# Spreading the LayerNorm factor over the partitions: two transfers through DRAM, or transposes on TensorE

## The reference, cut to what matters

```
xn     = (x - mean(x)) / sqrt(var(x) + 1e-5)              # per token (row)
q      = lora_proj(xn, Wq...);  k, v = lora_proj(ctx, ...) # 16 heads of 16
scores = q*0.25 @ k^T + bias                               # bias: [128, 16, 128, 128] f32
x      = x + tanh(g_xattn) * softmax(scores) @ v
t      = layernorm(x);  e = argmax(softmax(t @ Wg + bg))   # one of 8 experts
x      = x + tanh(g_ffn) * (gelu(t @ W1[e] + b1[e]) @ W2[e] + b2[e])
```

## Time and profile before

| | |
|---|---|
| time, median of 3 runs (lowest, highest) | 2027.51 us (2027.22, 2029.68) |
| time of the profiled execution | 2017.96 us |
| its span, first to last instruction | 2016.1 us |
| mean granted TensorE clock | 0.835 of full speed |
| busy: PE, DVE, ACT, POOL | 69%, 48%, 38%, 49% |
| DMA, mean over the span | 143 GB/s |

### The profile page before, as it was taken

One profiled execution on the slowest core, in us unless ns is written; L12 is line 12 of the kernel. 1 busy time (PEld: TensorE's weight loads), 2 busy tenths in 40 slices (PEclk: granted clock), 3 DMA queues, 4 the chain that ended last, 5 costly groups with the idle time before them and its releaser, 6 DMA issues.

```text
span 2016.1 us, 45866 instructions
## 1 busy us (share of the span) xinstructions
PE 1390.3 (69%) x12568; PEld 1158.6 (57%) x12568; DVE 974.1 (48%) x5961; ACT 772.7 (38%) x1660; POOL 997.8 (49%) x1051
## 2 busy tenths in 40 slices
PE   5656666676766666766656666767665666999998
PEld 3445545554655455555545555656554555788887
DVE  3334445443544444444444444545444444756555
ACT  1334434343433343443333343434333343533333
POOL 2334545554545445554445444545445445655555
PEclk7778878888877788877878887878787888999999
DMA  4454556555556565566556555665555654688896
GB/s 113 125 119 126 132 126 132 101 130 131 131 111 123 127 122 113 124 131 131 111 122 131 129 114 116 130 131 131 125 111 129 127 115 107 214 289 281 276 284 215
DMA packets 156795, 289.27 MB, mean 143 GB/s; under 512 B 36836, under 2 KB 72166, under 8 KB 156544
## 3 DMA queue, kind: packets, MB, share of 16 engines
q1 hardware_dynamic: 142992, 252.02, 55.1%
q0 software_dynamic: 12624, 34.62, 4.6%
q10 hardware_dynamic: 1056, 1.39, 0.2%
HBM read 251.89 MB, written 36.98 MB: 143 GB/s over the span
## 4 chain that ended last, share of the span: by engine, by line
DMA 69%; PE 14%; SPq 9%; issue 6%; DVE 1%; ACT 0%; POOLq 0%; POOL 0%; DVEq 0%; ACTq 0%
DMA rs_dram<-x2n 68%; PE bank L788 6%; PE bank L802 6%; SPq L402 5%; SPq L366 2%; PE bank L776 1%; DMA x_sb<-in_x 1%; DMA RS<-rs_dram 1%; DVE sc L1042 1%; SPq L356 0%; PE bank L595 0%; PE bank L629 0%; PE bank L620 0%; SPq L384 0%; SPq L379 0%
## 5 line engine op out<-in xcount | busy, mean ns | idle before, releaser
L1042 DVE CUSTOM_DVE_ANT_0 sc<-bank,sc 128x128 f32<-128x128 f32 x2048 | 443.9, 286 | 264.3 <-PE bank L595 133.7
L484 POOL TENSOR_TENSOR sc<-sc,rowmax 128x1024 f32<-128x1024 f32 x256 | 480.0, 1896 | 156.9 <-DVE rowmax L1042 148.7
L595 PE MATMUL bank<-KT,QT 32*128 32x256 f32 x2048 | 195.6, 509 | 476.0 <-DVE QT L1101 443.9
L595 PEld LDWEIGHTS bank<-KT,QT 32*128 32x128 f32 x2048 | 119.7, 238 | 511.5 <-DVE QT L1101 373.3
L506 POOL TENSOR_SCALAR ve<-mv 128x2 f32<-128x2 f32 (+1 forms) x135 | 31.5, 233 | 674.3 <-DVE mv L1065 649.9
L620 PE MATMUL bank<-cst,sc 128*128 128x128 f32 x2048 | 291.6, 289 | 1.2 <-issue 1.2
L886 ACT ACTIVATE PT<-bank 128x512 f32<-128x512 f32 x512 | 281.6, 604 | 17.6 <-PE bank L620 14.1
L620 PEld LDWEIGHTS bank<-cst,sc 128*128 128x128 f32 x2048 | 243.2, 149 | 35.0 <-issue 34.7
L1052 DVE BATCH_NORM_STATS2 st<-x_sb 128x6 f32<-128x256 f32 x128 | 53.7, 419 | 399.6 <-DMA x_sb<-in_x 399.5
L852 ACT ACTIVATE QT<-QT,cst 128x256 f32<-128x256 f32 x128 | 58.0, 501 | 444.8 <-DVE QT L1101 444.8
L645 PE MATMUL bank<-XT,wq 128*128 128x256 f32 x512 | 148.0, 439 | 115.0 <-DVE rowmax L1042 114.5
(11 more groups left out here) (148 smaller groups left out, 2157.1 us busy)
## 6 DMA issues: line engine op xcount, KB each, us to landing
sc<-in_bias SPq DMA_DIRECT2D x256, 512.0 KB
w_sb<-in_w SPq DMA_DIRECT2D x69, 257.0 KB, 3.9
CT<-in_w SPq DMA_DIRECT2D x69, 256.0 KB, 4.0
xg<-rows_dram SPq DMA_DIRECT2D x63, 272.0 KB, 3.9
x_sb<-in_x SPq DMA_DIRECT2D x128, 128.0 KB, 11.1
CT<-in_ctx_in SPq DMA_DIRECT2D x64, 256.0 KB
XT<-in_x_turned SPq DMA_DIRECT2D x64, 256.0 KB
RS<-rs_dram SPq DMA_DIRECT2D x128, 64.0 KB
```

Source lines behind the costliest of these rows:

```text
L484: nc.gpsimd.tensor_tensor(s, s, m, ALU.subtract).then_inc(sub_ok, 1)
L595: ins = mm(b_s[j][:, 2 * P * c:2 * P * c + 2 * P], QT[rows, pair, c, P * sq:P * sq + P], KT[rows, pair, c, sq].rearrange("p e k -> p (e k) ...
L1042: ins = nc.vector.tensor_tensor_reduce(out=s, in0=b_s[q][:, P * (h % 4):P * (h % 4) + P], in1=s, scale=1.0, scalar=LOWEST, op0=ALU.add, op ...
```

## The change

The two transfers, the DRAM tensor rs_dram and the semaphores rs_out and rs_in go. In each even step TensorE makes two transposes, for the two sequences of the pair, of the factor's column repeated 128 times (a broadcast access pattern), into the second half of bank b_x, once the semaphore rs_ok says that GpSimd has written both factors. ScalarE copies the 128x256 result to RS, which now has one buffer. V, which uses the same bank, waits for that copy (rs_evac), and so does `scale_queries`.

```diff
-            def send_scale(t):
-                sp.wait_ge(rs_ok, t.n(1, 1))
-                sp.nop(nofuse=True)
-                sp.dma_start(rs_dram[t.n()], ln[:, (t.k - 7) % 8, 0, 0:1]).then_inc(rs_out, 16)
-
-            def spread_scale(t):
-                pair = t.k // 2 % 2
-                if t.reached(4):
-                    sp.wait_ge(scaled_ok, t.per(2, 1, -1))
-                    sp.nop(nofuse=True)
-                sp.wait_ge(rs_out, t.n(16, 16))
-                sp.nop(nofuse=True)
-                tok = P * t.slot(2)
-                sp.dma_start(RS[:, pair, tok:tok + P], rs_rows[t.n()].partition_broadcast(P)).then_inc(rs_in[pair], 16)
...
@@ PE, step @@
+                if qry and qry.slot(2) == 0:
+                    pe.wait_ge(rs_ok, qry.n(1, 2))
+                    if not cur and val.reached(1):
+                        pe.wait_ge(v_evac, val.n())
+                    for n in range(2):
+                        rs = ln[:, (qry.k + n - 7) % 8, 0, 0:1].broadcast_to([P, P])
+                        ins = nc.tensor.transpose(b_rs[:, P * n:P * n + P], rs, ident)
+                    ins.then_inc(rs_ready, 1)
...
-                    if not cur and val.reached(1):
+                    if qry and qry.slot(2) == 0:
+                        pe.wait_ge(rs_evac, qry.per(2, 1, 1))
+                    elif not cur and val.reached(1):
                         pe.wait_ge(v_evac, val.n())
@@ ACT, step @@
+                if qry and qry.slot(2) == 0:
+                    act.wait_ge(rs_ready, qry.per(2, 1, 1))
+                    nc.scalar.copy(RS[:], b_rs).then_inc(rs_evac, 1)
@@ DVE, scale_queries @@
-                dve.wait_ge(rs_in[pair], t.per(4, 32, 32))
+                dve.wait_ge(rs_evac, t.per(2, 1, 1))
```

More of the change, by code:

```diff
@@ L106, in sem @@
             return ctx.enter_context(nc.semaphore(name))
-        rs_dram = nc.dram_tensor("rs_dram", (N, P, 1), F32, kind="Internal").ap()
-        rs_rows = rs_dram.rearrange("n p a -> n a p")
         rows_dram = nc.dram_tensor("rows_dram", (DUMMY + FT, ROW), F32, kind="Internal").ap()
@@ L136, in flamingo_block @@
         sc = sb("sc", [P, 4, HEADS * P])
-        RS = sb("RS", [P, 2, 2 * P])
+        RS = sb("RS", [P, 2 * P])
         XT = sb("XT", [P, 2, KC, 2 * P])
@@ L201, in flamingo_block @@
         b_x, b_o = bank[6], bank[7]
-        b_v, b_x2 = b_x[:, 0:HID], b_s[3]
+        b_v, b_rs, b_x2 = b_x[:, 0:HID], b_x[:, HID:HID + 2 * P], b_s[3]
         o_ps = b_o[:].rearrange("p (h c) -> p h c", c=CELL)
@@ L253, in flamingo_block @@
         xT_in = [sem(f"xT_in{i}") for i in range(2)]
-        rs_out, rs_in = sem("rs_out"), [sem(f"rs_in{i}") for i in range(2)]
+        rs_ready, rs_evac = sem("rs_ready"), sem("rs_evac")
         s_setc, scaled_ok = sem("s_setc"), sem("scaled_ok")
@@ L351, in _ @@
             load(cst[:, 0:C_FIRST], consts[:, 0:C_FIRST], s_id)
-            def send_scale(t):
-                sp.wait_ge(rs_ok, t.n(1, 1))
-                sp.nop(nofuse=True)
-                sp.dma_start(rs_dram[t.n()], ln[:, (t.k - 7) % 8, 0, 0:1]).then_inc(rs_out, 16)
-            def spread_scale(t):
-                pair = t.k // 2 % 2
-                if t.reached(4):
-                    sp.wait_ge(scaled_ok, t.per(2, 1, -1))
-                    sp.nop(nofuse=True)
-                sp.wait_ge(rs_out, t.n(16, 16))
-                sp.nop(nofuse=True)
-                tok = P * t.slot(2)
-                sp.dma_start(RS[:, pair, tok:tok + P], rs_rows[t.n()].partition_broadcast(P)).then_inc(rs_in[pair], 16)
             def step(i, k):
                 behind = seq(i, k, -4)
-                if behind and not (isinstance(i, int) and k < 0):
-                    send_scale(behind)
                 t = seq(i, k, -6) if k > FIRST else None
@@ L389, in step @@
                     sp.dma_start(XT[:, behind.k // 2 % 2], x_turned[behind.per(2)]).then_inc(xT_in[behind.k // 2 % 2], 16)
[L390 to L393, removed]
                 t = seq(i, k, -3)
@@ L1097, in scale_queries @@
                 pair = t.k // 2 % 2
-                dve.wait_ge(rs_in[pair], t.per(4, 32, 32))
+                dve.wait_ge(rs_evac, t.per(2, 1, 1))
                 for o in range(KC):
                     dve.wait_ge(q_ready, t.per(2, KC, o + 1))
-                    ins = nc.vector.tensor_tensor(QT[:, pair, o, :], b_s[o][:, 0:2 * P], RS[:, pair, :], ALU.mult)
+                    ins = nc.vector.tensor_tensor(QT[:, pair, o, :], b_s[o][:, 0:2 * P], RS[:], ALU.mult)
                 ins.then_inc(scaled_ok, 1)
```

## The result

The changed kernel takes 1321.72 us, median of 4 runs (1308.79 to 1326.63), against 2027.37 us of the kernel before (4 runs). The ratio is 0.651, with a 95% interval of 0.646 to 0.656. The forecast was 1360, in 1300 to 1510. The profiled execution took 1308.79 us, its span is 1307.0.

What follows compares the result with a forecast made beforehand. TensorE (PE) was to bound the kernel at 7.9 us per step. First scores 23 + 127 x 7.9 + code waits 36 + end 292 = 1354 span, 1356 with 1.9 outside, 1363 as median, called 1360; range 1300 to 1510.

Steps and rivals of the forecast that it cites:

- its row of 7.89: TensorE's odd step between two scores with hardly a wait, 7.89 us at full clock, including the gating logits.
- first scores: Start of the kernel: without the early transfers' waits, the first scores move from 37.58 to about 23 us.
- 127 steps: First to last scores: TensorE's 7.60 us plus 0.19 for transposes, 7.8, plus 0.1 for small waits, 7.9 us each.
- code waits at the heads: VectorE's waits without a releaser where its loop jumps back, read as code fetch: 3 us, 12 times, 36 us.
- after the last scores: Stretch from the last scores to the end, without such transfers: stays at 291.9 us.
- the quick value, 3.9, less 1 of slack: Price of one head wait: x's quick landing of 3.9 us, less about 1 of VectorE's slack, 3 us.
- The wait of SyncE: SyncE stood 1161.2 us in 125 waits for the factor's send, 9.3 us each; removal would not win all.
- the loop of x: Rival: loading x, with landing time L, sets the step; 1977 us at L 11.1, some 1585 at 8; chance 0.14.
- the isolated send of 8.98 us: First send, ahead of the first bias load: 8.98 us, read as the trip being slow for itself, not queued.
- The rule on the fixed cost: About 2 us per transfer, 254 us in 127 steps for the send; the prediction said the trace disagrees.
- V's wait for the copy of RS: V waits for ScalarE's new copy in the shared bank: margin 0.7 us, cost nothing, 64 us at most.
- the rival of a slow clock: Rival: TensorE without pauses still gets the low clock, a step of 14.2 us, some 2130 us; chance 0.03.

Runs made afterwards that it cites:

- the repeated one: The changed kernel itself, unaltered, measured again beside the kernel before at 1960.44 us: 1324.92 us, ratio 0.675.

## Why the prediction was right

**The bound after the change** was named rightly: PE, at full clock, about the 7.8 us per step that its row of 7.89 gave. Term by term, against the profiled span of 1307.0 where the sum said 1354:

| term | predicted | measured |
|---|---|---|
| first scores | 23 | 19.9 |
| 127 steps | 127 x 7.9 = 1003 | 956, by the steps without a wait |
| code waits at the heads | 12 x 3 = 36 | about 10, by the start times |
| copies held up | not in the sum | about 26, by the start times |
| after the last scores | 292 | 295.8 |

The start times give, in steps with no wait, 7.23 for a plain odd step, 7.45 for a plain even one, 7.55 with the counts and 7.89 with the logits: a mean of 7.53. The prediction's 7.79 was too high in two prices. The two transposes were put at the 0.38 us of a row, which is a duration, and cost 0.22 to 0.25 between starts. The logits were put at 0.46, the first of their two pieces (the second is the transposes of their result), and cost 0.66, the distance from 7.23 to 7.89. The 0.1 added for small waits was not needed. These prices and that of the head waits made the sum 73 us too long, and the held up copies, which it did not have, gave 26 back: that much of the nearness of 1360 to 1321.72 is luck.

**The head waits** were seen and rightly read as VectorE's code: they went when the loop was written out. Their price, "the quick value, 3.9, less 1 of slack", was too high. The wait itself was sized well: the seven that stand out in the profiled run are 3.1 to 3.7 us long, where 3.9 was taken. What was too small is the slack that hides it. In the run with the writes apart, where no copies are held up, that step takes 8.54 in place of 7.45, so 1.1 us each. The slow send is what made them long: in the run with the constant send side by side they are 6.6 to 10.1 us, with the writes apart 3.1 to 3.4.

**The wait of SyncE** was rightly read as being on the path: the chain of the kernel before lies 68% on it, and that of the run with send and wait 53%. What the prediction left open is that the wait is only one face of the send's cost. "Per step one send, one read back and the wait of 9.3 us" took the three away as one item. The runs part them: the send costs about 500 us though nobody waits for it, through its neighbours, above all the scatter (landing in 10.3 us with it, in 4.7 with the writes apart). The prediction had "the trip also makes its neighbours late, or seems to" and the loop of x as a rival with L; it had nothing on the scatter. In the kernel before VectorE stood 399.5 us for x and GpSimd 24.0 us for the scatter; which loop would have held it without the wait, no run isolates. These loops did not outlive the change, because the change took the send away. Had the change only moved the wait, the prediction would have been wrong by 500 us or more, as the late read back shows. The one row that spoke for itself was the isolated send of 8.98 us with x at 3.9 in front of it; x had been issued ahead of the send there, so the row could not tell whether those behind it suffer.

**The rule on the fixed cost**, 2 us per transfer by the page "DMA: Bandwidth & Descriptors" of the Trainium skill (Anatomy of one DMA, for transfers issued by GpSimd), agrees with x once the send is gone (2.0 us, issued by SyncE). Summed as a price for the send it would have given 1770 for the changed kernel, 450 too many.

**V's wait for the copy of RS** and the copy itself cost nothing that the rows show: V follows the projection at once. **The clock** stood at 1.00 in the loop; the rival of a slow clock had no support. **The step's own residue**, the held up copy, was nowhere in the prediction; it is about 26 us of 1307 in the profiled run and about 38 in the repeated one. Two signs were off with it or beside it: the steps lie 7.2 to 9.1 us apart in the full stretch, not 7.4 to 8.1, and x lands in 2.0 us, not 4 to 6.

## What to carry to other kernels

A long wait for a transfer on an issuing queue is not yet a price. Ask whether the transfer only is late, or makes those around it late: put the transfer alone into the other kernel. Hiding the wait alone says less, since it can bring another wait in its place, as the late read back did. If a chain runs through a tiny transfer with the DMA engines busy at low GB/s, look at where its bytes land. When an engine becomes the bound, take prices from the distance between starts in a full stretch, since durations overlap.

## What the runs showed of the hardware

- 128 writes of 4 bytes into one 512-byte stretch of DRAM per step cost this kernel about 525 us in 128 steps (1808.14 us against 1282.8 with the writes 512 bytes apart; one run each), and doubled the landing of an unrelated scatter (10.3 against 4.7 us). 128 writes of 512 bytes cost nothing (1284.71).
- In the changed kernel, ScalarE's copy out of PSUM starts 0.4 to 1.2 us after the matmuls that it waits for, in place of 0.06 to 0.14, when the issue of an indirect DMA on GpSimd, 1.06 us long, begins 0.06 to 1.22 us before their end (46 of 46 cases, and none of the other 71). Making the scatter wait took the time from 1324.92 to 1294.13 us, 1.8% by the ratios. VectorE's instructions beside the issue kept their pace (0.29 us each). In the run with the writes apart the same overlap delayed no copy (20 cases), so it is not the whole cause; what the two share is not shown.
- At the head of each of 12 rounds of its loop VectorE waits with no releaser: 3.1 to 3.4 us with the writes apart, 1.1 us of it on the path, and 6.9 to 12.1 us in the kernel before, beside the slow writes. With the loop written out these waits are gone. That they are the fetch of code is inferred from this.
